# Reordering the per-block work of ScalarE and VectorE in the projection stage of a fused conditional-residual kernel

## Chip, cores and metric

The kernel runs on one core of one Trainium2 chip. The metric is the device time of one execution in microseconds. TensorE is PE, VectorE is DVE, ScalarE is ACT, GpSimd is POOL; SyncE (SP) issues most of the DMAs.

## The reference, cut to what matters

An activation `x` of shape (64, 32, 512) goes through four residual layers. The first three are small mixers. The fourth is paged attention with 32 query heads and 8 key and value heads of 128, and its projections are the stage that is changed:

```python
q = rmsnorm(x @ Wq.T) ; k = rmsnorm(x @ Wk.T) ; v = x @ Wv.T   # 4096, 1024 and 1024 columns
q, k = rope(q, pos), rope(k, pos)
o = softmax(q @ concat(k_cache, k).T / sqrt(128), masked) @ concat(v_cache, v)
x = x + o @ Wo.T
```

## The kernel before, in words

The program has three stages, one after the other: the mixers, the projections, and the attention. The function `projections` works on 16 tiles of 128 rows of `x`. Every tile is multiplied with 12 column blocks of 512: steps 0 to 7 are queries, 8 and 9 keys (steps 0 to 9 are those "with rotation", `ROT` = 10), and 10 and 11 values (`BLK` = 12). Numbers are kept as pairs of 16-bit parts, so a block costs 12 matmuls into one of four PSUM banks `blk` (L963 to L965).

Each engine has its own hand-written order, a loop over the steps n of a tile (`body`, L878, L955, L1024, L1110, L1226), and the engines meet at counting semaphores. What one block goes through:

- PE: the 12 matmuls; then `turn_heads` (L934), four transposes into a PSUM bank `tq` of heads that were finished two steps before. The heads turned at step n are query block n-2, and at steps 0 and 1 the two key blocks of the tile before. `tq` and its SBUF target `turned` have two buffers each, used in turn, so even steps and odd steps have one each. After block 10 PE runs `turn_x` (L923), which transposes the next tile's input.
- ACT: waits for block n, takes the row sums of squares (`squares`, L994, four instructions with accumulators at L999), and then in the same step copies the heads turned at step n-1 to `turned` as the high 16-bit part (`heads_high`, L986, executed at L979). Before that copy it waits until the DMA that stored the previous contents of the same `turned` buffer has landed (`out_q`). At even steps it splits a piece of the key cache, value cache or output weight (`chunk_high`, L1017). At steps 0 and 1 it scales the key blocks of the tile before (`normalise_keys`, L1003) before it waits for the block. At step 8 it makes the high part of the next tile's input (`x_high`, L981).
- DVE: waits for the squares of block n (both engines read the same PSUM bank, so one goes after the other), makes the two rotary products (`rotate`, L1208 and L1212), then the low part of the heads turned at step n-1 (`heads_low`, L1218), at odd steps the low part of the piece (`chunk_low`, L1223), one of eight small steps on the next tile's scales (`scale_step`, L1134), at step 9 `x_low` (L1163), and at step 10 `keep_xt` (L1168), which takes the transposed input out of PSUM. `mean` (L1172), a square root on ACT (L1028) and `inverse` (L1185 to L1194) close the tile.
- POOL: adds the two products (`add`, L1087), some work on the values (L1092, L1097), and at step 8 the tables of the next tile (L1071).
- SP: at even steps stores the piece whose `chunk_low` DVE made in the step before and loads another (`chunks`, L864; the store waits for `c_low`), and only then stores the heads turned at step n-2 (`store_heads`, L826). At step 9 it stores the values of the tile before (L847).

Of the kernel before, what the change touches and what calls it, by code (L numbers as in the profile page):

```python
# [696 lines left out]
def projections(nc, ident, ident16, up, cs, vw, cos, sin, wa, wb, wh, wl, first, v_idx, pages, wo_t, k_t, v_rows,  # L697
# [4 lines left out]
    with ctx:  # L702
# [36 lines left out]
        out_q = [sem(f"stored{i}") for i in range(2)]  # L739
        rest1, vmid, vlow, v_out = sem("v_rest"), sem("v_mid"), sem("v_low"), sem("v_stored")  # L740
        XSTEPS, CSTEPS, CHUNKS = 7, 4, 6

        keys0, query0, values0, fresh0, rscale0, page_row = first
        pages_in, early, early_values = sem("pages_in"), sem("first_sample"), sem("first_values")
# [58 lines left out]
        def is_tile(t, n):  # L803

            return isinstance(t, int) and t == n
# [113 lines left out]
        @block.tensor  # L919
        def _(pe):  # L920
            mm = nc.tensor.matmul

            def turn_x(t, p):  # L923

                pe.wait_ge(xhigh, t + 1)
                pe.wait_ge(xlow, t + 1)
                after(pe, xt_done, t)
                for k in range(KD):
                    for h, part in enumerate((xh, xl)):
                        at = (2 * k + h) * P  # L930
                        last = nc.tensor.transpose(xp[:, at:at + P], part[:, k * P:(k + 1) * P], ident16[:, :])
                last.then_inc(xturned, 1)

            def turn_heads(t, n):  # L934
                idx = t * ROT + n
                if n < QB:
                    pe.wait_ge(sum_done, idx + 1)
                    src = rn[n % NR]
                else:
                    pe.wait_ge(kn_done, t * KB + n - QB + 1)  # L940
                    src = kr[n - QB]
                after(pe, high, idx - 1)
                after(pe, low, idx - 1)
                for h in range(HB):
                    last = nc.tensor.transpose(tq[n % 2][:, h * P:(h + 1) * P], src[:, h * P:(h + 1) * P],
                                               ident[:, :])
                last.then_inc(tq_done, 1)

            def bank_free(t, n):
                if n < ROT:  # L950
                    pe.wait_ge(rot_done, t * ROT + n + 1)
                else:
                    pe.wait_ge(v_read, t * VB + n - ROT + 1)

            def body(t, p):  # L955
                pe.wait_ge(xt_done, t + 1)
                for n in range(BLK):
                    if unread(t, n):
                        bank_free(*unread(t, n))
                    out = blk[n % NB][:, :]  # L960
                    cols = slice(n * D, (n + 1) * D)
                    for k in range(KD):
                        mm(out, xt[p][:, k, 0, :], wh[:, k, cols], start=(k == 0), stop=False)  # L963
                        mm(out, xt[p][:, k, 0, :], wl[:, k, cols], start=False, stop=False)  # L964
                        last = mm(out, xt[p][:, k, 1, :], wh[:, k, cols], start=False, stop=(k == KD - 1))  # L965
                    last.then_inc(blk_done, 1)
                    if heads_at(t, n):
                        turn_heads(*heads_at(t, n))
                    if n == ROT and not is_tile(t, NT - 1):
                        turn_x(t + 1, 1 - p)  # L970

            turn_x(0, 0)
            tiles(pe, body)
            for n in range(QB, ROT):
                turn_heads(NT - 1, n)

        @block.scalar
        def _(act):
            copy = lambda out, in_, **kw: nc.scalar.activation(out, in_, ACT.Copy, **kw)  # L979

            def x_high(t, p):  # L981
                act.wait_ge(scaled, t + 1)
                after(act, xturned, t)
                copy(xh[:, :], x3[p][:, :], scale=col[p][:, 2:3]).then_inc(xhigh, 1)

            def heads_high(t, n):  # L986
                idx = t * ROT + n
                act.wait_ge(tq_done, idx + 1)

                after(act, out_q[n % 2], count(t, n) * 16)  # L990
                src, dst, _ = head_views(n)
                copy(dst, src).then_inc(high, 1)

            def squares(t, n):  # L994

                after(act, sq_done, t * ROT + n - 1)
                for h in range(HB):
                    at = h * QB + n if n < QB else HQ + (n - QB) * HB + h
                    last = nc.scalar.activation(square[n % 2][:, h, :], blk[n % NB][:, h * HD:(h + 1) * HD], ACT.Square,  # L999
                                                accum_out=ss[:, 0, at:at + 1])  # L1000
                last.then_inc(sq_done, 1)

            def normalise_keys(t, p, j):  # L1003
                act.wait_ge(sum_done, t * ROT + QB + j + 1)
                act.wait_ge(inv_done, t + 1)
                for h in range(HB):
                    cols = slice(h * HD, (h + 1) * HD)
                    at = HQ + j * HB + h
                    last = copy(kr[j][:, cols], kr[j][:, cols], scale=inv[p][:, at:at + 1])
                last.then_inc(kn_done, 1)  # L1010

            def middle(t, j):

                act.wait_ge(rest1, t * VB + j + 1)
                copy(vp[:, 1, j * D:(j + 1) * D], v32[j][:, :]).then_inc(vmid, 1)

            def chunk_high(t, c):  # L1017
                act.wait_ge(c_in[c % 3], t * (16 * CHUNKS // 3) + (c // 3 + 1) * 16)

                after(act, c_out[c % 3], t * (16 * CHUNKS // 3) + c // 3 * 16)  # L1020
                a, h, _ = chunk_views(c)
                copy(h, a, scale=up[:, c // 2:c // 2 + 1]).then_inc(c_high, 1)

            def body(t, p):  # L1024
                for n in range(BLK):
                    if n == BLK - 1:
                        act.wait_ge(root_in, t + 1)
                        nc.scalar.activation(ss[:, 2, :], ss[:, 1, :], ACT.Sqrt).then_inc(rooted, 1)  # L1028
                    if not is_tile(t, 0) and n < KB:
                        normalise_keys(t - 1, 1 - p, n)  # L1030
                    act.wait_ge(blk_done, t * BLK + n + 1)
                    if n < ROT:
                        if n == 0:
                            after(act, root_in, t)
                        squares(t, n)
                    if heads_at(t, n - 1):
                        heads_high(*heads_at(t, n - 1))
                    if not is_tile(t, 0) and n in (2, 4):
                        middle(t - 1, n // 2 - 1)
                    if n % 2 == 0:  # L1040
                        chunk_high(t, n // 2)
                    if n >= ROT:
                        j = n - ROT

                        after(act, v_out, t * 4 * 16)
                        after(act, vlow, t * VB)
                        copy(v32[j][:, :], blk[n % NB][:, :], scale=col[p][:, 6:7])
                        copy(vp[:, 0, j * D:(j + 1) * D], blk[n % NB][:, :], scale=col[p][:, 6:7]
                             ).then_inc(v_read, 1)
                    if n == ROT - 2 and not is_tile(t, NT - 1):  # L1050
                        x_high(t + 1, 1 - p)

            x_high(0, 0)
            tiles(act, body)
            for j in range(KB):
                normalise_keys(NT - 1, 1, j)
            for j in range(KB):
                heads_high(NT - 1, QB + j)
            for j in range(VB):
                middle(NT - 1, j)  # L1060
# [70 lines left out]
        def _(dve):  # L1131
# [93 lines left out]

            def body(t, p):  # L1226
                for n in range(BLK):
                    if n < ROT:
                        rotate(t, p, n)
                    if heads_at(t, n - 1):  # L1230
                        heads_low(*heads_at(t, n - 1))
                    if n % 2 == 1:
                        chunk_low(t, n // 2)
                    if not is_tile(t, NT - 1):
                        if n <= XSTEPS:
                            scale_step(t + 1, 1 - p, n)
                        if n == ROT - 1:
                            x_low(t + 1, 1 - p)
                        if n == ROT:
                            keep_xt(t + 1, 1 - p)  # L1240
                    if n == ROT:
                        mean(t, p)
                    if n == BLK - 1:
                        inverse(t, p)
# [462 lines left out]
```

## Time and profile before

| | us |
|---|---|
| median of 3 runs (2423.46 to 2427.11) | 2425.59 |
| the profiled execution, its own time | 2425.75 |
| its span, first to last instruction | 2424.1 |
| PE busy in the span | 2172.3 (90%) |
| DVE busy | 1985.7 (82%) |
| ACT busy | 1408.3 (58%) |
| POOL busy | 1042.5 (43%) |

The lines of the profile are read like this: the line number is that of the kernel file, then come the engine and the operation, "out<-in" by the program's buffer names, and the shape. Rows of a timeline begin with the start and the duration in us, and end, where the engine had been idle, with how long and what released it. PE's busy time is longer than its issue time, since matmuls overlap, so PE can wait although it shows as busy.

### The profile page before, as it was taken

The numbers are of one execution on the slowest core, as the hardware profiler recorded it, in microseconds if no ns is written. First come the engines' busy times: TensorE is split into PE (matmuls) and PEld (weight loads), VectorE is DVE, ScalarE is ACT, GpSimd is POOL, SyncE is SP. The second block draws the span as 40 slices with busy tenths as digits, with TensorE's granted clock in tenths as the row PEclk, the third lists the DMA queues.
The fourth block names the chain that finished last, engine by engine and source line by source line (L and its number), as shares of the span: only waits on it lengthen the run. The fifth ranks groups of instructions, "written<-read, shape, count | busy, mean of one in ns | idle before, by whom it ended". The sixth has DMA issues, their size and how long they took to land.

```text
span 2424.1 us, 61876 instructions
## 1 busy us (share of the span) xinstructions
PE 2172.3 (90%) x17328; PEld 1376.8 (57%) x17328; DVE 1985.7 (82%) x5085; ACT 1408.3 (58%) x4073; POOL 1042.5 (43%) x1329
## 2 busy tenths in 40 slices
PE   0886889899998975899999999999999999999998
PEld 0443444444444433666666666676676666766765
DVE  7786767767676766899998998998998998998995
ACT  0443666666666664566665665665665665665663
POOL 3343444444444443344444443443443444444442
PEclk9998999999999998999999999999999999999999
DMA  7884454545454559977777877877877777777771
GB/s 278 309 301 153 139 179 160 188 149 180 161 173 161 169 195 304 304 217 235 238 234 214 242 234 216 240 232 216 240 234 222 234 232 224 235 229 230 238 230 53
DMA packets 402151, 522.68 MB, mean 216 GB/s; under 512 B 50866, under 2 KB 297522, under 8 KB 399795
## 3 DMA queue, kind: packets, MB, share of 16 engines
q1 hardware_dynamic: 361010, 371.71, 48.9%
q0 software_dynamic: 40832, 147.34, 19.2%
q8 instruction: 135, 2.21, 0.4%
q14 instruction: 174, 1.42, 0.2%
HBM read 426.36 MB, written 92.54 MB: 214 GB/s over the span
## 4 chain that ended last, share of the span: by engine, by line
issue 26%; PE 20%; POOL 9%; DVE 4%; SPq 1%; POOLq 1%; DMA 1%; DVEq 0%; ACT 0%; ACTq 0%
PE att_y L1504 5%; PE att_scores L1464 5%; POOL wh L1410 4%; PE att_tr L1472 3%; POOL att_values L1401 3%; PE att_o L1492 2%; PE att_o L1493 2%; PE att_o L1494 2%; POOL wh L1401 1%; DVE att_prob L1590 1%; PE att_tr_new L1475 1%; POOL att_ot L1418 1%; DMA wh<-k_parts 1%; SPq L95 1%; DVE att_tpl L1613 1%
## 5 line engine op out<-in xcount | busy, mean ns | idle before, releaser
L1532 ACT ACTIVATE att_tph<-att_tr 128x512 f16<-128x512 f32 x512 | 305.8, 597 | 516.4 <-PE att_tr_new L1475 516.4
L1590 DVE CUSTOM_DVE_ANT_0 att_prob<-att_scores,att_mask 128x544 f32<-128x544 f32 x512 | 371.0, 725 | 106.7 <-PE att_scores L1465 65.6
L1410 POOL TENSOR_TENSOR wh<-att_prob,att_col 128x128 f32<-128x128 f32 x512 | 230.5, 450 | 524.7 <-DVE att_col L1601 500.2
L1504 PE MATMUL att_y<-att_wo,att_ot 128*128 128x512 f16 x1536 | 408.6, 380 | 5.9 <-DVE att_res L1630 5.9
L1613 DVE SCALAR_TENSOR_TENSOR att_tpl<-att_tr,att_tph 128x512 f16<-128x512 f32 x512 | 347.6, 679 | 2.5 <-ACT att_tph L1532 1.7
L1472 PE MATMUL att_tr<-ident,wh 128*128 128x128 f32 x2048 | 329.2, 284 | 0.8 <-DVE wh L1606 0.8
L1606 DVE TENSOR_SCALAR wh<-att_prob,att_col 128x512 f32<-128x512 f32 x512 | 327.5, 640 | 0.0
L1087 POOL TENSOR_TENSOR proj_rn<-proj_ra,proj_rb 128x512 f32<-128x512 f32 x128 | 162.7, 1271 | 320.2 <-DVE proj_rb L1212 320.2
L963 PE MATMUL proj_blk<-wh,proj_xt 128*128 128x512 f16 x768 | 294.8, 384 | 0.8 <-DVE proj_xt L1168 0.8
L964 PE MATMUL proj_blk<-wl,proj_xt 128*128 128x512 f16 x768 | 294.9, 384 | 0.0
L965 PE MATMUL proj_blk<-wh,proj_xt 128*128 128x512 f16 x768 | 294.9, 384 | 0.0
L1464 PE MATMUL att_scores<-wh 128*128 128x512 f16 x768 | 228.2, 387 | 51.6 <-PEq L702 20.4
L1208 DVE TENSOR_TENSOR proj_ra<-proj_blk,proj_ta 128x512 f32<-128x512 f32 x160 | 110.0, 687 | 180.2 <-ACT proj_square L999 180.2
L1418 POOL TENSOR_TENSOR att_ot<-att_of,att_ot 128x512 bf16<-128x512 f32 x128 | 158.4, 1238 | 225.3 <-DVE att_ot L1625 209.7
L1472 PEld LDWEIGHTS att_tr<-ident,wh 128*128 128x128 f32 x2048 | 217.6, 142 | 63.9 <-issue 2.8
L999 ACT ACTIVATE proj_square<-proj_blk 128x128 f32<-128x128 f32 x640 | 168.5, 278 | 130.8 <-PE proj_blk L965 130.5
L1536 ACT ACTIVATE att_prob<-att_prob,att_col,att_rscale 128x544 f32<-128x544 f32 x256 | 215.3, 841 | 32.8 <-DVE att_col L1596 20.7
L1536 ACT ACTIVATE att_prob<-att_prob,att_col,rscale 128x544 f32<-128x544 f32 x256 | 215.4, 841 | 27.8 <-DVE att_col L1596 18.6
L1464 PE MATMUL att_scores<-att_keys,att_query 128*128 128x512 f16 x768 | 220.9, 378 | 2.2 <-DVE att_col L1590 1.4
L1504 PEld LDWEIGHTS att_y<-att_wo,att_ot 128*128 128x128 bf16 x1536 | 153.8, 101 | 85.5 <-issue 9.5
L1492 PE MATMUL att_o<-att_tph,att_values 128*128 128x128 f16 x1024 | 188.9, 222 | 2.8 <-DMA att_values<-v_parts,att_idx 1.7
L1493 PE MATMUL att_o<-att_tpl,att_values 128*128 128x128 f16 x1024 | 188.7, 222 | 0.0
(195 smaller groups left out, 5329.4 us busy)
## 6 DMA issues: line engine op xcount, KB each, us to landing
wh<-k_parts SPq DMA_DIRECT2D x512, 128.0 KB, 4.3
att_keys<-k_parts SPq DMA_DIRECT2D x512, 128.0 KB
q_parts<-proj_turned SPq DMA_DIRECT2D x128, 256.0 KB, 2.9
v_new_parts<-proj_vp SPq DMA_DIRECT2D x64, 256.0 KB, 3.0
wh<-q_parts SPq DMA_DIRECT2D x32, 512.0 KB, 4.9
att_query<-q_parts SPq DMA_DIRECT2D x32, 512.0 KB
pro_ring<-in_w_t SPq DMA_DIRECT2D x12, 1024.0 KB, 8.3
mix_wraw<-in_w_t POOLq DMA_DIRECT2D x24, 512.0 KB, 5.6
```

Of the source, the lines that this page charges most:

```text
L963: mm(out, xt[p][:, k, 0, :], wh[:, k, cols], start=(k == 0), stop=False)
L964: mm(out, xt[p][:, k, 0, :], wl[:, k, cols], start=False, stop=False)
L965: last = mm(out, xt[p][:, k, 1, :], wh[:, k, cols], start=False, stop=(k == KD - 1))
L1410: g.tensor_tensor(norm[q][:, L:L + P].rearrange("p (a s) -> p a s", s=S), prob[q][:, cached(q)[1]].unsqueeze(1).to_broadcast([P, 4, S]), c ...
L1464: mm(old, a, k, start=start, stop=stop)
L1472: nc.tensor.transpose(tr[q][:, c * P:(c + 1) * P], norm[q][:, c * P:(c + 1) * P], ident[:, :])
L1504: last = mm(y_ps[:, :], ot[p][:, a, h, :], wo[:, h, w, :], start=(h == 0 and start), stop=(h == HQ - 1 and stop))
L1532: copy = lambda out, in_, **kw: nc.scalar.activation(out, in_, ACT.Copy, **kw)
L1536: nc.scalar.activation(prob[q][:, :], prob[q][:, :], ACT.Exp, bias=col[q][:, 1:2], scale=row_scale(i), accum_out=col[q][:, 2:3]).then_inc( ...
L1590: v.tensor_tensor_reduce(out=prob[q][:, :], in0=sc[q], in1=mask[bi % 2][:, at:at + LK], scale=1.0, scalar=-3.0e38, op0=ALU.add, op1=ALU.ma ...
L1606: v.tensor_scalar(out=norm[q][:, 0:L], in0=prob[q][:, cached(q)[0]], scalar1=col[q][:, 3:4], scalar2=None, op0=ALU.mult).then_inc(norm_don ...
L1613: v.scalar_tensor_tensor(out=tpl[q][:, :], in0=tr[q][:, :], scalar=TOP, in1=tph[q][:, 0:L], op0=ALU.mult, op1=ALU.subtract)
```

## The change

Three moves, and nothing is added or taken away. On ACT `heads_high` of step n-1 stands ahead of the wait for block n and its squares instead of behind them, and `x_high` of the next tile stands at step 5, in front of that wait, instead of at the end of step 8. On DVE `heads_low` stands ahead of `rotate`, two scale steps of the next tile are made in each of steps 0 to 3 instead of one in each of 0 to 7, `x_low` comes at step 6, and all of these stand ahead of `rotate`; `chunk_low` stays behind it. On PE `turn_x` follows block 9 instead of block 10.

```diff
+        XHIGH = 5
 ...
                     if heads_at(t, n):
                         turn_heads(*heads_at(t, n))
-                    if n == ROT and not is_tile(t, NT - 1):
+                    if n == ROT - 1 and not is_tile(t, NT - 1):
                         turn_x(t + 1, 1 - p)
 ...
                         normalise_keys(t - 1, 1 - p, n)
+                    if heads_at(t, n - 1):
+                        heads_high(*heads_at(t, n - 1))
+                    if n == XHIGH and not is_tile(t, NT - 1):
+                        x_high(t + 1, 1 - p)
                     act.wait_ge(blk_done, t * BLK + n + 1)
                     if n < ROT:
                         if n == 0:
                             after(act, root_in, t)
                         squares(t, n)
-                    if heads_at(t, n - 1):
-                        heads_high(*heads_at(t, n - 1))
 ...
-                    if n == ROT - 2 and not is_tile(t, NT - 1):
-                        x_high(t + 1, 1 - p)
 ...
                 for n in range(BLK):
-                    if n < ROT:
-                        rotate(t, p, n)
                     if heads_at(t, n - 1):
                         heads_low(*heads_at(t, n - 1))
-                    if n % 2 == 1:
-                        chunk_low(t, n // 2)
                     if not is_tile(t, NT - 1):
-                        if n <= XSTEPS:
-                            scale_step(t + 1, 1 - p, n)
-                        if n == ROT - 1:
+                        for step in range(2 * n, min(2 * n + 2, XSTEPS + 1)):
+                            scale_step(t + 1, 1 - p, step)
+                        if n == XHIGH + 1:
                             x_low(t + 1, 1 - p)
                         if n == ROT:
                             keep_xt(t + 1, 1 - p)
+                    if n < ROT:
+                        rotate(t, p, n)
+                    if n % 2 == 1:
+                        chunk_low(t, n // 2)
                     if n == ROT:
                         mean(t, p)
```

## Rows read from the trace of the kernel before

**Rows 1.** Windows; columns: stretch, us, busy us (instructions) per engine, PE clock, DMA.
```profile
228.00:859.00 631.00, 569.81 (x2871) 278.55 (x2872) 439.84 (x790) 403.69 (x1667) 285.80 (x270) 0.98 0.50 165
```
**Rows 2.** Waits from 228 to 899 us; columns: total us, times, longest.
```profile
DVE proj_ra L1208 <- ACT proj_square L999: 180.2, 97, 6.6
...
ACT proj_turned L979 <- DMA q_parts<-proj_turned: 34.6, 49, 2.1
PE proj_xp L931 <- issue: 32.5, 15, 2.3
...
ACT proj_turned L979 <- DMA k_new_parts<-proj_turned: 22.0, 15, 1.8
```
**Rows 3.** Tiles proj_xp, proj_xh and line L1223; columns: ns minimum/median/maximum, first and last start.
```profile
L1168 DVE COPY proj_xt<-proj_xp x16: 691/692/693, 227.2 to 856.9; 128x1024 f16<-128x1024 f16 x16
...
L979 ACT ACTIVATE proj_xh<-proj_x,proj_col x16: 710/744/753, 224.5 to 849.8; 128x512 f16<-128x512 f32 x16
...
L1223 DVE SCALAR_TENSOR_TENSOR proj_chunk_parts<-proj_chunk,up,proj_chunk_parts x96: 739/1214/1465, 238.3 to 897.6; 128x512 f16<-128x512 f32 x96
```
**Rows 4.** Timeline of one tile, steps 5 to 9: from one stored piece to the next.
```profile
590.80 1.38 DVE L1223 SCALAR_TENSOR_TENSOR proj_chunk_parts<-proj_chunk,up,proj_chunk_parts 128x512 f16<-128x512 f32 x1
...
592.21 0.33 SPq L861 DMA_DIRECT2D v_parts<-proj_chunk_parts  x1
...
593.41 1.24 SPq L839 DMA_DIRECT2D q_parts<-proj_turned  x2
...
596.25 0.60 ACT L979 ACTIVATE proj_turned<-proj_tq 128x512 f16<-128x512 f32 x1 [0.74 <-DMA q_parts<-proj_turned]
...
596.88 0.69 DVE L1218 TENSOR_TENSOR proj_turned<-proj_tq,proj_turned 128x512 f16<-128x512 f32 x1
...
597.49 1.24 DVE L1223 SCALAR_TENSOR_TENSOR proj_chunk_parts<-proj_chunk,up,proj_chunk_parts 128x512 f16<-128x512 f32 x1
...
602.97 0.60 ACT L979 ACTIVATE proj_turned<-proj_tq 128x512 f16<-128x512 f32 x1 [0.77 <-DMA q_parts<-proj_turned]
```
**Rows 5.** Timeline: squares, products and sum of step 7, transposes of steps 8 and 9.
```profile
594.37 0.28 ACT L999 ACTIVATE proj_square<-proj_blk 128x128 f32<-128x128 f32 x1 [1.27 <-PE proj_blk L965]
...
595.54 0.69 DVE L1208 TENSOR_TENSOR proj_ra<-proj_blk,proj_ta 128x512 f32<-128x512 f32 x1 [0.68 <-ACT proj_square L999]
...
596.15 0.68 DVE L1212 TENSOR_TENSOR proj_rb<-proj_blk,proj_tb 128x512 f32<-128x512 f32 x1
...
596.91 1.27 POOL L1087 TENSOR_TENSOR proj_rn<-proj_ra,proj_rb 128x512 f32<-128x512 f32 x1 [0.95 <-DVE proj_rb L1212]
...
597.72 0.63 PE L945 MATMUL proj_tq<-ident,proj_rn 128*128 128x128 f32 x4 [0.26 <-DVE proj_turned L1218]
...
600.79 0.63 PE L945 MATMUL proj_tq<-ident,proj_rn 128*128 128x128 f32 x4
```
**Rows 6.** Timeline of the same tile, steps 2 and 3: the first heads.
```profile
579.92 1.12 SPq L839 DMA_DIRECT2D k_new_parts<-proj_turned  x2
...
583.02 0.60 ACT L979 ACTIVATE proj_turned<-proj_tq 128x512 f16<-128x512 f32 x1 [1.28 <-DMA k_new_parts<-proj_turned]
```
**Rows 7.** Timeline of the same tile: its first steps, and steps 9 to 0 of the next.
```profile
570.80 0.63 PE L945 MATMUL proj_tq<-ident,proj_kr 128*128 128x128 f32 x4
...
572.44 1.28 ACT L979 ACTIVATE proj_kr<-proj_kr,proj_inv 128x128 f32<-128x128 f32 x4
...
601.05 0.28 ACT L999 ACTIVATE proj_square<-proj_blk 128x128 f32<-128x128 f32 x1 [0.63 <-PE proj_blk L965]
...
606.90 0.69 DVE L1168 COPY proj_xt<-proj_xp 128x1024 f16<-128x1024 f16 x1
...
607.51 0.23 DVE L1172 TENSOR_SCALAR proj_ss<-proj_ss,proj_col 128x40 f32<-128x40 f32 x1
...
609.79 0.16 DVE L1194 TENSOR_TENSOR proj_inv<-proj_ss 128x8 f32<-128x8 f32 x1
...
611.97 0.66 PE L945 MATMUL proj_tq<-ident,proj_kr 128*128 128x128 f32 x4
```

## The prediction

> **What bounds the kernel now.** The change touches one stage, so I first cut the trace to it. In the windows view the steady part of the projections lasts 631 us, with PE busy 570, DVE 440, ACT 404 and POOL 286 [rows 1]. No engine is full, so what matters is who waits for whom. The copy of the transposed input gives the cadence: L1168 runs 16 times from 227.2 to 856.9, so a tile takes 629.7 / 15 = 41.98 us [rows 3]. PE alone could do better: two successive transposes of heads with a full block between them, in a stretch where nothing held the second, start 3.07 us apart (597.72 to 600.79) [rows 5]. Ten such steps and two blocks without transposes would be some 36 us. So about 6 us a tile are waiting.
>
> The list of waits shows where. PE stands 32.5 us in 15 waits, 2.2 us a tile, ahead of the transposes of the next input (L931) [rows 2]. DVE waits 180 us for the squares, and ACT 34.6 + 22.0 us for the DMA that stores turned heads [rows 2]. The DMA waits are the ones to look at, since they repeat with a period of their own. I followed one even step to the next in the timeline [rows 4]: the low part of the piece, L1223, ends at 590.80 + 1.38 = 592.18. SP, which had been waiting for it, stores the piece at 592.21, loads another, and only then, at 593.41, stores the heads. That store lands and lets ACT take the next even heads at 596.25. DVE follows at 596.88, L1223 at 597.49 to 598.73, and the next heads leave at 602.97. Hence a loop of 602.97 - 596.25 = 6.72 us for two steps, against 2 x 3.07 = 6.14 us for PE. **This loop of stores, not PE, sets the pace of the steady steps**, and PE shows it: its transposes at 597.72 had waited 0.26 us for the low part of the heads [rows 5]. The squares are outside the loop, because they stand ahead of the head copy on ACT: in the same step the squares began at 594.37, 1.9 us before the copy at 596.25 [rows 4, 5].
>
> **The change, part by part.** I write S for the start of a step's squares and H for the start of the copy of heads in front of them in the new order. All instructions stay, so only order counts.
>
> *Heads ahead of the squares (ACT).* ACT works in order. The copy H still waits for the store of the heads two steps back, and now the squares are queued behind that wait, and behind the squares the products on DVE, and behind those L1223, and behind L1223 on SP the store that the next H waits for. The loop is closed through the squares. Its length:
> - S to the first product 595.54 - 594.37 = 1.17; to the second 0.61; DVE is free again after another 0.61 (as between 596.88 and 597.49); L1223 at its undisturbed 0.74 [rows 3 to 5]. Together 3.13 us from S to the end of L1223. The low part of the heads costs nothing here: it runs beside the squares (0.69 us against 1.17).
> - End of L1223 to H: 596.25 - 592.18 = 4.07 in one loop and 602.97 - 598.73 = 4.24 in the next [rows 4]; I take 4.15. For the first pair the store is that of keys, whose issue to copy is 583.02 - 579.92 = 3.10 against 596.25 - 593.41 = 2.84 [rows 4, 6], so 4.4.
> - H to the squares 0.60 [rows 4].
>
> That is 3.13 + 4.15 + 0.60 = **7.88 us for two steps, where 6.72 stand now**; 8.13 for the pair with the keys' store. PE's 6.14 hides under it, as does POOL's sum (1.27) with the transposes behind it.
>
> *The input's high part at step 5* (`x_high`) stands between a late H and the squares of step 5. Its 0.74 [rows 3] was beside PE's work before; now it is in the loop once per tile. 7.88 + 0.74 = 8.62.
>
> *From the tile's first transposes to the squares of step 1*: the key scaling starts at 572.44 and takes 1.28 as now, and then the heads of step 0 leave (0.60) ahead of the squares: 574.3 - 570.80 = 3.5 us [rows 7].
>
> *From the squares of step 1 to those of step 9*: 8.13 + 8.62 + 7.88 + 7.88 = 32.5 us.
>
> *The end of the tile.* Today the squares of step 9 start at 601.05 and the first transposes of the next tile at 611.97, 10.9 us later, with PE's wait of 2.2 us for the input inside [rows 7, 2]. In the new order the input has been split since step 6 and is turned after block 9, so this wait goes. What is late next is the copy of the input out of PSUM: DVE does products and L1223 of step 9 (3.13 after S), the low heads (0.61), the copy (0.61 to the next start, 606.90 to 607.51), so `mean` starts at 4.4. `Mean` to the end of `inverse` is 609.95 - 607.51 = 2.44, then comes the key scaling at 1.28 and some 0.1 of hand-over: 8.2 us after S [rows 7]. PE's next block starts when the copy is done, at about 4.4, and ends at 7.0, so the key scaling ends last. **The tile's end gains 2.7 us.**
>
> *Scale steps by two, and the low part of the input at step 6* cost nothing as long as they run while DVE waits for squares. Without that cover the low part adds its own duration, 0.74 like L1223's minimum, once a tile; the even step it is in has over a microsecond free.
>
> Sum for a tile: 3.5 + 32.5 + 8.2 = 44.2 against 41.98, +2.2 us. Fourteen full tiles: +31. The first tile has no keys' store ahead of it and so one loop less, about 0. In the last tile (whose input part at step 5 falls away) there is no input wait to win back: today its squares of step 9 come 30.25 us after the first transposes (601.05 - 570.80) [rows 7], in the new order 3.5 + 31.8 = 35.3, so +5. Together +36 on the profiled execution's 2425.75: **2462 us**. Its span lies 1.7 us under that, and the time 0.2 us above the median of the runs, so nothing is to be corrected.
>
> **The price from both sides.** L1223 can be 0.74 or up to 1.47 [rows 3]. In the rows it is long when POOL's sum runs: POOL from 596.91 to 598.18, L1223 until 598.73, some 0.55 after POOL's end [rows 4, 5]. In these rows the two did not overlap. In the new order L1223 comes right behind the second product, 0.61 after its start, and POOL's sum 0.76 after it; L1223 would be first by 0.15 us. I take it as first, with POOL's sum half a microsecond later, under cover. If POOL wins, L1223 ends 0.76 + 1.27 + 0.55 = 2.58 after the second product rather than 1.35: +1.23 in each of four loops. For the store's landing the rows give 2.84 to 3.10.
>
> The Trainium skill (SBUF — State Buffer, "Who interferes with whom") says of the port that DVE and POOL share that issue order decides who blocks, and the first holds it for its whole instruction. By that rule L1223 keeps its 0.74 and the sum stays 2462; by the longest measured duration it would be the second rival. The rows before agree with the rule for the POOL-first order alone.
>
> A difference under 0.2%, about 5 us, cannot be told from no change.
>
> **The rivals.**
> 1. *POOL gets the port first.* 1.23 x 4 = 4.9 us a tile, x 16 = 79: 2541. Against it are the 0.15 us above; for it, that this lead is small. 8%.
> 2. *The opposite sign: the head copies are never late.* Then the squares keep today's spacing and the tile's end gains 2.7 us x 15 = 40: 2385. This needs the store to land before the block is done: from the end of L1223 only 6.14 - 3.13 - 0.60 = 2.4 us remain, and 4.07 is the shortest I saw. For it: stores issued at another moment meet other transfers, and DMA is busy only half of the time [rows 1]. 11%.
> 3. *Loss and gain cancel.* Shortening each of four loops by 0.55 us takes the 2.2 us away, i.e. a way from L1223 to copy of 3.6 us: about 2425. 7%.
> 4. *The clock.* The mean granted clock of the stage is 0.98 of 2.4 GHz [rows 1], so little time is spent at the lower level of 1.2 GHz. In the new order PE idles over a microsecond in every second step, and if that brought more time at the lower level, a block of 2.6 us would cost as much again at most; most of it lies under the loop. It would add up to 30 us and stays inside my forecast's own range.
>
> **How the numbers follow.** The loop through the squares, with port and clock uncertain, has 74%, and 2440 to 2495 as its own range. Faster is rival 2, 12% with a part of rival 3; same is the rest of rival 3, 6%; slower is the loop and rival 1, 82%. The range 2424 to 2510 leaves out rivals 1 and 2.
>
> **What would show it.** In the changed profile the wait of PE ahead of L931 is gone; ACT's waits for the stores of heads grow from 57 us to well over 100, and the squares start right behind a head copy at steps 3, 5, 7 and 9; the head copies of even steps are 7.9 us apart (today 6.72); L1223 takes 0.74 in most places; the copy L1168 is spaced by about 44 us. If the copies are 6.2 us apart and L1168 by less than 40, the store was never in the way and I am wrong. If L1223 stays at 1.2 or more, rival 1 holds.

## The result, and the profile after

The changed kernel takes **2470.38 us** (median of 4 runs, 2466.41 to 2475.03) against 2426.05 us, a ratio of 1.0185 with a 95% interval of 1.0165 to 1.0205: 44 us slower, where 36 us slower (2462 us) had been forecast. The time lies inside the stated range of 2424 to 2510 us. The profiled execution has a span of 2467.8 us.

The three windows below are those of the projections' steady part, of the last tile with the tail, and of the rest, in the changed kernel.

```profile
226.90:888.80 661.90, 567.75 (x2873) 280.57 (x2874) 411.73 (x787) 390.22 (x1665) 310.38 (x270) 0.99 0.47 156
888.80:939.60 50.80, 40.37 (x192) 20.23 (x192) 28.21 (x53) 31.47 (x126) 22.11 (x17) 0.93 0.46 158
939.60:2467.80 1528.20, 1435.99 (x13824) 1011.39 (x13824) 1339.20 (x3795) 899.21 (x2179) 650.94 (x963) 0.98 0.76 228
```

The steady part took 631 us [rows 1] and takes 662 now; PE, DVE and ACT are busy for as long as before or less. POOL's busy time alone grew, from 286 to 310 us. So the time is waiting. The list of waits from 228 to 945 us says for whom:

```profile
DVE proj_turned L1219 <- ACT proj_turned L980: 196.5, 80, 5.4
ACT proj_turned L980 <- DMA q_parts<-proj_turned: 191.7, 59, 6.1
...
DVE proj_ra L1209 <- ACT proj_square L1000: 62.7, 93, 5.9
PE proj_tq L946 <- DVE proj_turned L1219: 47.1, 40, 3.6
...
ACT proj_turned L980 <- DMA k_new_parts<-proj_turned: 36.7, 15, 2.7
```

ACT's wait for the stores of turned heads went from 34.6 + 22.0 [rows 2] to 191.7 + 36.7 = 228 us. The wait of PE ahead of the transposes of the next input, 32.5 us before [rows 2], is not in the list any more. The change took away the wait it was aimed at, and it made the wait for the stores four times as long.

Next the two tiles views, with the copy of the transposed input and the low part of the pieces, to be held against [rows 3]:

```profile
L1169 DVE COPY proj_xt<-proj_xp x16: 677/679/691, 226.1 to 888.0; 128x1024 f16<-128x1024 f16 x16
...
L1224 DVE SCALAR_TENSOR_TENSOR proj_chunk_parts<-proj_chunk,up,proj_chunk_parts x96: 739/742/745, 237.3 to 932.4; 128x512 f16<-128x512 f32 x96
...
L1088 POOL TENSOR_TENSOR proj_rn<-proj_ra,proj_rb x128: 1261/1450/1714, 234.8 to 924.1; 128x512 f32<-128x512 f32 x128
```

A tile takes (888.0 - 226.1) / 15 = 44.13 us instead of 41.98. The low part of the piece is never longer than 745 ns, and POOL's sum is longer instead (median 1450 ns, 1267 before).

The timeline of steps 5 to 9 of one tile shows the loop, in the place of [rows 4, 5]:

```profile
602.88 0.60 ACT L980 ACTIVATE proj_turned<-proj_tq 128x512 f16<-128x512 f32 x1 [3.60 <-DMA q_parts<-proj_turned]
...
603.98 0.27 ACT L1000 ACTIVATE proj_square<-proj_blk 128x128 f32<-128x128 f32 x1
604.35 0.63 PE L946 MATMUL proj_tq<-ident,proj_rn 128*128 128x128 f32 x4 [1.31 <-DVE proj_turned L1219]
...
605.15 0.69 DVE L1209 TENSOR_TENSOR proj_ra<-proj_blk,proj_ta 128x512 f32<-128x512 f32 x1 [0.95 <-ACT proj_square L1000]
605.76 0.68 DVE L1213 TENSOR_TENSOR proj_rb<-proj_blk,proj_tb 128x512 f32<-128x512 f32 x1
606.36 0.74 DVE L1224 SCALAR_TENSOR_TENSOR proj_chunk_parts<-proj_chunk,up,proj_chunk_parts 128x512 f16<-128x512 f32 x1
606.52 1.71 POOL L1088 TENSOR_TENSOR proj_rn<-proj_ra,proj_rb 128x512 f32<-128x512 f32 x1 [3.65 <-DVE proj_rb L1213]
607.12 0.33 SPq L862 DMA_DIRECT2D v_parts<-proj_chunk_parts  x1
...
608.33 0.98 SPq L840 DMA_DIRECT2D q_parts<-proj_turned  x2
611.22 0.60 ACT L980 ACTIVATE proj_turned<-proj_tq 128x512 f16<-128x512 f32 x1 [3.46 <-DMA q_parts<-proj_turned]
...
618.96 0.60 ACT L980 ACTIVATE proj_turned<-proj_tq 128x512 f16<-128x512 f32 x1 [3.98 <-DMA q_parts<-proj_turned]
619.45 0.27 ACT L1000 ACTIVATE proj_square<-proj_blk 128x128 f32<-128x128 f32 x1
623.09 0.68 DVE L1169 COPY proj_xt<-proj_xp 128x1024 f16<-128x1024 f16 x1
...
627.54 0.66 PE L946 MATMUL proj_tq<-ident,proj_kr 128*128 128x128 f32 x4 [0.88 <-ACT proj_kr L980]
```

Read it from the top: the copy of heads starts once the old store has landed, after 3.6 us in which ACT did nothing; then the squares, the products, the low part of the piece, its store, the store of the heads, and again a copy that waited 3.46 us. From copy to copy it is 8.34 us with the input's high part in between, and 7.74 us in the next pair.

Not all of the 44 us is here. The attention stage starts with L1464 at 923.8 us before and with L1465 at 958.1 after, and the rest to the end of the span is 1500.3 and 1509.7 us:

```profile
L1464 PE MATMUL att_scores<-wh x768: 376/377/634, 923.8 to 2366.9; 128*128 128x512 f16 x192
...
L1630 DVE SCALAR_TENSOR_TENSOR att_res<-att_y,oscale,att_res x16: 750/751/752, 1112.1 to 2420.8; 128x512 f32<-128x512 f32 x16
```
```profile
L1465 PE MATMUL att_scores<-wh x768: 376/377/634, 958.1 to 2412.1; 128*128 128x512 f16 x192
...
L1631 DVE SCALAR_TENSOR_TENSOR att_res<-att_y,oscale,att_res x16: 750/751/752, 1144.9 to 2464.4; 128x512 f32<-128x512 f32 x16
```

The first fence is the kernel before, the second the changed one. The projections cost 34.3 us more and the attention, of which no line was changed, 9.4 us. Between the first and the last residual sum of the attention (`att_res`) it is 1308.7 us before and 1319.5 after.

### The profile page after: what moved, and what is told of

It is laid out like the page before. It is cut to its first block, busy times and chain, and to the rows that moved or that the text cites. A ratio compares the mean times of both kernels' runs of the same rounds, so it can differ in the third digit from the quotient of the medians.

```text
span 2467.8 us, 61864 instructions
## 1 busy us (share of the span) xinstructions
PE 2176.4 (88%) x17328; PEld 1381.6 (56%) x17328; DVE 1956.0 (79%) x5085; ACT 1396.7 (57%) x4073; POOL 1070.5 (43%) x1329
## 4 chain that ended last, share of the span: by engine, by line
issue 27%; PE 17%; POOL 9%; DVE 6%; POOLq 1%; SPq 1%; DMA 1%; DVEq 0%; ACT 0%
PE att_y L1505 5%; PE att_scores L1465 4%; POOL wh L1411 4%; POOL att_values L1402 3%; PE att_tr L1473 3%; DVE att_prob L1591 2%; POOL wh L1402 1%; PE att_o L1493 1%; PE att_o L1495 1%; PE att_o L1494 1%; PE att_tr_new L1476 1%; DVE att_tpl L1614 1%; POOL att_ot L1419 1%; DVE wh L1607 1%; DVE att_tph L1617 1%
## 5 line engine op out<-in xcount | busy, mean ns | idle before, releaser
L1591 DVE CUSTOM_DVE_ANT_0 att_prob<-att_scores,att_mask 128x544 f32<-128x544 f32 x512 | 370.8, 724 | 121.0 <-PE att_scores L1466 50.5
L1088 POOL TENSOR_TENSOR proj_rn<-proj_ra,proj_rb 128x512 f32<-128x512 f32 x128 | 189.3, 1479 | 322.4 <-DVE proj_rb L1213 310.4
L1465 PE MATMUL att_scores<-wh 128*128 128x512 f16 x768 | 226.6, 385 | 51.5 <-PEq L702 19.9
L1219 DVE TENSOR_TENSOR proj_turned<-proj_tq,proj_turned 128x512 f16<-128x512 f32 x160 | 109.9, 687 | 196.5 <-ACT proj_turned L980 196.5
L1465 PE MATMUL att_scores<-att_keys,att_query 128*128 128x512 f16 x768 | 222.2, 379 | 5.2 <-DMA att_keys<-k_parts 3.7
L980 ACT ACTIVATE proj_turned<-proj_tq 128x512 f16<-128x512 f32 x160 | 97.1, 607 | 229.0 <-DMA q_parts<-proj_turned 191.7
```

Of the source, the lines that this page charges most:

```text
L1465: mm(old, a, k, start=start, stop=stop)
L1591: v.tensor_tensor_reduce(out=prob[q][:, :], in0=sc[q], in1=mask[bi % 2][:, at:at + LK], scale=1.0, scalar=-3.0e38, op0=ALU.add, op1=ALU.ma ...
```

## Experiments

Two theories stood against each other for the projections: that a loop through the store of the heads, now with squares and products in it, sets the pace; or that the input's earlier split, or slow stores as such, are to blame. Four kernels came first, and the others followed from what they left open. The names of lines are those of the changed kernel; the kernel before has them one lower, and the kernels with added waits have the attention's two or three higher.

**SP's order in the changed kernel.**

```diff
                 for n in range(BLK):
-                    if n % 2 == 0:
-                        chunks(t, n // 2)
...
                     if heads_at(t, n - 2):
                         store_heads(*heads_at(t, n - 2))
+                    if n % 2 == 0:
+                        chunks(t, n // 2)
```

> The changed kernel with one edit on SP: at even steps the turned heads are stored before the piece, so their store no longer waits for L1224. Theory of the loop: from H the low heads end 1.3 us later, the store leaves at once and lands in 2.9 us, so the next copy could start 4.3 us after H, under PE's 6.14 us for two steps. The squares come on time, ACT's waits for the stores of heads fall from 228 us to under 30, a tile takes 36.5 to 38.5 us instead of 44.1, and the kernel 2426 - 15 x 4.5 = about 2355 us (2340 to 2385). Rival (the stores themselves are slow, by crowded DMA engines, and the order on SP is beside the point): waits and time stay near 2470, at most 10 us less.

Measured: 2350.56 us, ratio to before 0.9702 (0.9676 to 0.9729), some 120 us under the changed kernel with not one instruction more or less. The tiles view and the waits from 228 to 899 us:

```profile
L1169 DVE COPY proj_xt<-proj_xp x16: 678/680/692, 227.0 to 773.5; 128x1024 f16<-128x1024 f16 x16
```
```profile
ACT proj_turned L980 <- DMA q_parts<-proj_turned: 25.0, 43, 1.9
ACT proj_turned L980 <- DMA k_new_parts<-proj_turned: 12.0, 15, 2.4
```
```profile
575.32 1.88 SPq L840 DMA_DIRECT2D q_parts<-proj_turned  x2
575.89 0.60 PE L946 MATMUL proj_tq<-ident,proj_rn 128*128 128x128 f32 x4
...
578.13 0.60 ACT L980 ACTIVATE proj_turned<-proj_tq 128x512 f16<-128x512 f32 x1 [0.59 <-DMA q_parts<-proj_turned]
578.91 0.60 PE L946 MATMUL proj_tq<-ident,proj_rn 128*128 128x128 f32 x4
```

A tile takes 546.5 / 15 = 36.43 us, near the 36 us of PE's work, and PE's transposes are 578.91 - 575.89 = 3.02 us apart. The waits fell to 37 us, a little more than the 30 expected. Slow stores are ruled out: a store issued at 575.32 still let its copy start only at 578.13, 2.8 us later, as before, and it is when they are issued that counts.

**The same edit on the kernel before.**

> The kernel before with the same edit on SP alone. Theory: the loop of 6.72 us for two steps goes, steps run at PE's 3.07, and the 2.2 us wait for the next input stays: (6.72 - 6.14) x 4 = 2.3 us a tile less, 39.7 us a tile, about 2391 us (2380 to 2405). Rival (slow stores): 2426 within 5 us.

Measured: 2404.05 us, ratio 0.9926 (0.9898 to 0.9953). The direction is that of the loop, the size is below it: a tile takes (837.9 - 227.2) / 15 = 40.71 us, 1.3 less instead of 2.3. The waits for stores are nearly gone (6.4 and 0.2 us), but PE still waits 30.3 us ahead of the input's transposes. The rows of this kernel show why the gain is small:

```profile
573.74 0.63 PE L945 MATMUL proj_tq<-ident,proj_rn 128*128 128x128 f32 x4
...
576.21 0.68 DVE L1218 TENSOR_TENSOR proj_turned<-proj_tq,proj_turned 128x512 f16<-128x512 f32 x1
...
577.04 0.63 PE L945 MATMUL proj_tq<-ident,proj_rn 128*128 128x128 f32 x4
...
578.86 0.68 DVE L1212 TENSOR_TENSOR proj_rb<-proj_blk,proj_tb 128x512 f32<-128x512 f32 x1
579.45 0.68 DVE L1218 TENSOR_TENSOR proj_turned<-proj_tq,proj_turned 128x512 f16<-128x512 f32 x1
...
580.28 0.63 PE L945 MATMUL proj_tq<-ident,proj_rn 128*128 128x128 f32 x4
```

With no store in the way the transposes are still 3.30 and 3.24 us apart, 6.54 us for two steps and not 6.14. They start 0.15 us after the low heads have ended (576.21 + 0.68 = 576.89, then 577.04), and the low heads stand behind the products. So the old order holds a second loop, from PE's block over squares, products and low heads back to PE's transposes, a little shorter than the loop of stores. No run tests it by itself, but with the low heads ahead of the products, in the kernel above, the steps are at 3.02 us. The loop of stores in the kernel before is not much longer: its copies of even steps came at 583.02, 589.24, 596.25 and 602.97 [rows 4, 6], in the mean 6.65 us apart. The second of them is this row:

```profile
589.24 0.60 ACT L979 ACTIVATE proj_turned<-proj_tq 128x512 f16<-128x512 f32 x1 [0.27 <-DMA q_parts<-proj_turned]
```

**The input's moves alone** (the changed kernel with the heads back where they were):

```diff
-                    if heads_at(t, n - 1):
-                        heads_high(*heads_at(t, n - 1))
                     if n == XHIGH and not is_tile(t, NT - 1):
...
                         squares(t, n)
+                    if heads_at(t, n - 1):
+                        heads_high(*heads_at(t, n - 1))
...
-                    if heads_at(t, n - 1):
-                        heads_low(*heads_at(t, n - 1))
...
                         rotate(t, p, n)
+                    if heads_at(t, n - 1):
+                        heads_low(*heads_at(t, n - 1))
```

> The changed kernel with the head copies back behind the squares on ACT and the low heads back behind the products on DVE: what is left is the earlier splitting and turning of the next input. Theory: the loop is the old one, 6.72 us for two steps, and only the 2.2 us wait ahead of the input's transposes goes, of which 1.5 to 2.2 us a tile reach the end: 2426 - 25 = about 2400 us (2390 to 2410). Rival (the input's moves are what makes the change slow, by holding ACT and DVE in front of a block): 2440 or more.

Measured: 2417.33 us, ratio 0.9984 (0.9967 to 1.0001), so no difference clear of noise, and above the expected range (2390 to 2410). The projections did gain: (833.7 - 225.3) / 15 = 40.56 us a tile, 21 us over 15 tiles. The attention took 13 us back (1322.0 us between its residual sums against 1308.7), which is the miss. The input's moves are not what makes the change slow.

**The heads' moves alone** (on the kernel before):

```diff
+                    if heads_at(t, n - 1):
+                        heads_high(*heads_at(t, n - 1))
                     act.wait_ge(blk_done, t * BLK + n + 1)
...
                         squares(t, n)
-                    if heads_at(t, n - 1):
-                        heads_high(*heads_at(t, n - 1))
...
+                    if heads_at(t, n - 1):
+                        heads_low(*heads_at(t, n - 1))
                     if n < ROT:
                         rotate(t, p, n)
-                    if heads_at(t, n - 1):
-                        heads_low(*heads_at(t, n - 1))
```

> The kernel before with the heads' moves alone (copy ahead of the wait for the block on ACT, low part ahead of the products on DVE). Theory: the loop goes through the squares, 7.9 us for two steps, and the wait for the input at the end of the tile stays, so this is at least as slow as the whole change: 2470 to 2490 us, head copies of even steps 7.9 us apart. Rival (the input's moves are to blame): 2426 or less.

Measured: 2518.13 us, ratio 1.0402 (1.0365 to 1.0439): slower than the whole change by 48 us, more than the 20 allowed for. Head copies of even steps came at 577.72, 585.68, 593.37 and 601.28, 7.9 us apart as expected. What was too small was the price of the input at the end of the tile. In this kernel PE waits for it after block 10, by the timeline

```profile
606.66 0.22 PE L931 MATMUL proj_xp<-ident,proj_xh 128*128 128x128 f16 x1 [4.57 <-issue]
```

4.57 us and not 2.2: the low part of the input is behind a later step 9 on DVE, and took 1.75 us beside POOL's sum. The clock has a part in it too. The matmuls behind this wait start 0.43 us apart instead of 0.22, and the granted clock of the stage is 0.94 where the changed kernel has 0.99:

```profile
607.14 0.63 PE L963 MATMUL proj_blk<-wh,proj_xt 128*128 128x512 f16 x1
607.57 0.63 PE L964 MATMUL proj_blk<-wl,proj_xt 128*128 128x512 f16 x1
```
```profile
607.10:610.50 3.40, 3.40 (x11) 1.26 (x9) 2.79 (x10) 0.24 (x1) 0.00 (x0) 0.51 0.79 293
228.00:949.00 721.00, 594.86 (x2871) 288.12 (x2870) 433.14 (x793) 392.73 (x1668) 308.61 (x267) 0.94 0.44 145
```

Eight matmuls of that block take 3.4 us and not 1.7, and over the stage PE is busy for 595 us against 568 in the changed kernel, for the same matmuls. How much of these 27 us reached the end was not measured. The input's moves thus earn more inside the whole change than alone: they take away a wait which the heads' moves would have doubled.

**Which order, ACT's or DVE's.** Two kernels from the changed one: the low heads behind the products again (ACT's order is left), or the head copy behind the squares again (DVE's order is left).

```diff
-                    if heads_at(t, n - 1):
-                        heads_low(*heads_at(t, n - 1))
...
                         rotate(t, p, n)
+                    if heads_at(t, n - 1):
+                        heads_low(*heads_at(t, n - 1))
```

> The changed kernel with the low heads back behind the products on DVE, the head copy staying ahead of the squares on ACT. Theory: ACT's order alone closes the loop through the squares, and with the low heads between the products and L1224, POOL's sum now starts first and holds L1224 until 0.55 us after its end: 1.17 + 0.61 + 0.76 + 1.27 + 0.55 = 4.36 us from the squares to the end of L1224 instead of 3.13, so 9.1 us for two steps, 5 us a tile more than the change: 2540 us (2515 to 2560). Rival (ACT's order is harmless, DVE's does the damage): near 2420.

Measured: 2562.02 us, ratio 1.0562 (1.0536 to 1.0588), 2 us above the expected range. Here too the granted clock of the stage is 0.94, which the estimate had not counted. The price was worked out from POOL getting ahead, and both show: head copies at 595.70 and 604.72, 9.02 us apart, and L1224 at its long duration:

```profile
L1224 DVE SCALAR_TENSOR_TENSOR proj_chunk_parts<-proj_chunk,up,proj_chunk_parts x96: 737/1380/1468, 240.5 to 1029.0; 128x512 f16<-128x512 f32 x96
```

The other half:

```diff
-                    if heads_at(t, n - 1):
-                        heads_high(*heads_at(t, n - 1))
                     if n == XHIGH and not is_tile(t, NT - 1):
...
                         squares(t, n)
+                    if heads_at(t, n - 1):
+                        heads_high(*heads_at(t, n - 1))
```

> The changed kernel with the head copy back behind the squares on ACT, the low heads staying ahead of the products on DVE. Theory: the squares leave the loop but the products are in it: copy to low heads 0.63, 0.61 to the products, 1.22 for these, 0.74 for L1224, then 4.15 to the next copy, 7.35 us for two steps, between the 6.72 of before and the 7.88 of the change: 2440 us (2425 to 2455). Rival (DVE's order is harmless): near 2417, as with the input's moves alone; rival (DVE's order does all the damage): 2470.

Measured: 2465.95 us, ratio 1.0182 (1.0145 to 1.0219), a miss on the high side: as slow as the whole change. The loop is as short as expected (copies at 602.75, 610.12 and 617.57, 7.4 us apart), but the tile still takes (880.7 - 226.3) / 15 = 43.63 us. The estimate had left out the first pair, which runs from 594.83 to 602.75, 7.9 us. A further part is likely that the products of steps 2 and 9 now wait for a copy behind the squares; it was not measured apart. So either order closes a loop of its own: it takes both in their old places, or the store of the heads set free of the products, by SP's order as above or by DVE's as below.

**The piece ahead of the products** (the changed kernel, SP as it is):

```diff
                         heads_low(*heads_at(t, n - 1))
+                    if n % 2 == 1:
+                        chunk_low(t, n // 2)
...
-                    if n % 2 == 1:
-                        chunk_low(t, n // 2)
```

> The changed kernel with L1224, the low part of the piece, directly behind the low heads and ahead of the products on DVE; SP keeps its order. Theory: the store of the piece stays ahead of the store of the heads but no longer waits for squares and products: copy to low heads 0.63, 0.61, 0.74 for L1224, 4.15 to the next copy, 6.1 us for two steps, no more than PE's 6.14. Waits for stores of heads fall by more than half, a tile takes 37 to 39 us and the kernel about 2365 us (2350 to 2395). Rival (only SP's order counts): 2450 or more.

Measured: 2372.21 us, ratio 0.9776 (0.9743 to 0.9809); a tile takes (800.5 - 232.0) / 15 = 37.9 us. ACT's waits for the stores fell from 228 to 97.6 + 21.2 = 119 us, a little less than the half expected. With SP's order untouched, taking squares and products out of the loop is worth 98 us. The two kernels that open the loop in two different places both end far below the kernel before. That is the loop shown, not argued.

**The attention stage.** All kernels so far with the input's moves had the longer attention, and DVE's program in them, as built, is 2375 instructions long, in the others 2377. Waits on semaphores that have their value long before were put in once, ahead of DVE's first tile. In the built program the three waits are two instructions more here, and one more in the kernel before:

```diff
             keep_xt(0, 0)
+            dve.wait_ge(xlow, 1)
+            dve.wait_ge(xhigh, 1)
+            dve.wait_ge(scaled, 1)
             tiles(dve, body)
```

> The changed kernel with three waits that are long satisfied, once, on DVE ahead of its first tile; they bring DVE's program of 2375 instructions back to the 2377 of the kernel before. It asks about the attention stage, which the change does not touch: from the first to the last instruction of L1630 or L1631 it took 1308.7, 1308.3 and 1308.6 us in the three kernels with 2377 DVE instructions, and 1319.5, 1319.7 and 1322.0 in the three with 2375. Theory (where DVE's loop of the attention lies in its program sets a stall of instructions): 1308 to 1311 us there, and the kernel at 2458 to 2462. Rival (something else in the moved input work, or chance): 1319 to 1322 us there and the kernel near 2470.

Measured: 2459.14 us, ratio 1.0133 (1.0109 to 1.0156), 11 us under the changed kernel, with tiles of (891.7 - 229.3) / 15 = 44.16 us as before the edit. The residual sums, and DVE's waits without a releaser in this kernel's attention (from 1200 to 2440 us), then those of the changed kernel (from 1145 to 2465 us):

```profile
L1634 DVE SCALAR_TENSOR_TENSOR att_res<-att_y,oscale,att_res x16: 750/751/753, 1151.1 to 2458.6; 128x512 f32<-128x512 f32 x16
...
DVE att_mask L1579 <- issue: 13.1, 6, 2.8
DVE att_prob L1594 <- issue: 0.4, 2, 0.2
```
```profile
DVE att_prob L1591 <- issue: 30.0, 45, 4.5
DVE att_mask L1576 <- issue: 11.5, 6, 2.6
```

1307.5 us between the first and last residual sum, and the 30 us of waits at L1591 are gone. Two more kernels were run once each: the changed kernel with two of the three waits (2376 instructions), and the kernel before with all three (2378):

> The changed kernel with two satisfied waits, 2376 DVE instructions. One look at the same span: 1308 us or 1316 and more places the step between 2375 and 2377. The projections keep 44.1 us a tile.

> The kernel before with three satisfied waits once on DVE, so that its program has 2378 instructions, one more than before. One look at the attention's span from the first to the last residual sum. If only positions of 2375 stall (a boundary crossed by the shorter program), it stays at 1308 us; if every length but 2377 stalls, it is 1316 or more. The projections keep 42.0 us a tile either way.

With 2376 the attention took 2466.1 - 1145.1 = 1321.0 us and DVE stood still before L1578 for 34.0 us in 6 waits; with 2378 it took 2416.5 - 1112.0 = 1304.5. The single times were 2471.04 and 2421.52 us, and the tiles took 44.0 and 42.0 us. By these single runs the step is between 2376 and 2377 instructions.

**Both findings together**: the changed kernel with SP's order and the three waits.

> The changed kernel with both findings: SP stores the turned heads ahead of the piece, and DVE's program is brought to 2377 instructions by satisfied waits. If both effects are what they seem and add up: tiles at 36.4 us as with SP's order alone, the attention's L1630 to L1634 rows spanning 1308 us instead of 1319.7, the kernel 2350.6 - 11 = 2340 us (2335 to 2346). If the attention's stall belongs to something else: 2350.

Measured: **2335.61 us**, ratio to before 0.9643 (0.9626 to 0.966), the fastest of all: tiles of (775.9 - 228.9) / 15 = 36.5 us and an attention of 2337.3 - 1029.2 = 1308.1.

```profile
ACT proj_turned L980 <- DMA q_parts<-proj_turned: 26.8, 43, 2.5
ACT proj_turned L980 <- DMA k_new_parts<-proj_turned: 11.0, 15, 2.4
```

## Why the prediction was right, and where it was off

- **What bounds the kernel.** The loop of stores, 6.72 us for two steps, was said to set the pace. SP's order on the kernel before takes its waits away, but gains 1.3 us a tile and not 2.3. Two sizes were off. The 6.72 us is one pair of steps, and the mean of three pairs in that tile is 6.65. And PE's own pace, 3.07 us a step, is not what the old order falls back to without the waits for stores: it runs at 3.27, since another loop, of 6.54 us, lay close under the loop of stores.
- **The loop through squares and products.** Forecast 7.88 us; the rows show 7.74, and 8.34 with the input's high part in it where 8.62 was forecast. Its parts fit: squares to first product 1.17 us; squares to the end of L1224 607.10 - 603.98 = 3.12 (3.13 forecast); from there to the next copy 4.12 (4.15); copy to squares 0.49 where 0.60 was taken, since ACT starts its next instruction before the last has ended.
- **The end of the tile.** 627.54 - 619.45 = 8.09 us against the 8.2 forecast.
- **The tile.** 44.13 us in the mean against 44.2. The tile shown takes less: its first transposes are at 584.16 and the squares of step 1 at 587.42, so with 619.45 - 587.42 = 32.03 up to those of step 9 it is 3.26 + 32.03 + 8.09 = 43.38 us where 3.5 + 32.5 + 8.2 stood. Each term is a little too long for this tile, and that the mean is met to 0.1 us is in part luck.
- **Port between DVE and POOL.** L1224 came first by 0.16 us (606.36 against 606.52) and kept its 0.74 everywhere. POOL's sum took 1.71 us instead of 1.27 and so paid 0.44 us, which stayed under cover. The rows before showed POOL first only; the changed kernel shows DVE first, and now both orders agree with what the Trainium skill (SBUF — State Buffer, "Who interferes with whom") says, that who issues first blocks the other. In the kernel with ACT's order alone, POOL is first again (598.73 against 599.17), and L1224 takes 1.38 us instead of 0.74. That is about half of what a loop is longer there (9.02 us against 7.74); the other 0.6 us are the low heads between the products and L1224.
- **Rivals.** POOL first (2541, once called "the second rival" in the prediction) did not come. Its mechanism showed in the kernel with ACT's order alone, which ran at 2562. That head copies are never late (2385) failed in the changed kernel; with SP's order it is nearly so, at 2351. In the changed kernel the clock moved little: 0.99 in the steady windows, 0.93 in the last tile with the tail. In the two slower kernels, the heads' moves alone and ACT's order alone, it fell to 0.94 over the stage.
- **The term that was missing.** The sum held +36 us for the projections and nothing for what follows; they gave +34.3, and 9.4 came from the attention, through DVE's program being two instructions shorter. The step that failed is that the prediction put nothing for the stages behind the one it changed; "All instructions stay, so only order counts" was the sentence: the computing instructions stay, the waits between them are laid down differently. With the length restored the kernel is at 2459, 32 to 35 us over before (ratio 1.0133, medians 2459.14 and 2424.55), near the 36 forecast.

## What to carry to other kernels

Before a step is moved ahead of a wait, write down the loop that the wait belongs to: which buffer, which store, and what the queue that issues this store is itself waiting for. Here the store of the heads stood behind a store that depended on DVE's last work of the step, and the move put the squares and products into that loop; two lines moved on SP turned 44 us of loss into some 72 us of gain (ratio 0.9702). Neither part does it alone: SP's order without the moves gave 18 us (ratio 0.9926). And look at the stages that a change does not touch: a few us there can be an effect of the program's length, which satisfied waits can test cheaply.

## What was not expected of the hardware

With 2375 or 2376 instructions in DVE's program the attention took 1315.5 to 1322.0 us between its residual sums in seven kernels; with 2377 or 2378 it took 1304.5 to 1308.7 in six. In the long ones DVE stands still with no releaser in the profile: the longest such wait is 4.0 to 5.2 us with 2375 instructions (at L1591) and 6.0 us with 2376 (at the line of the mask). In the short ones it is 3.0 us at most. The changed kernel's timeline has such a place about once in two tiles, of which this is one:

```profile
1320.95 0.43 DVE L1626 CAST att_ot<-att_of 128x512 bf16<-128x512 f32 x1
1323.31 0.66 DVE L1576 TENSOR_SCALAR att_mask<-att_iota,lens_f 128x512 f32<-128x512 f16 x1 [1.93 <-issue]
1327.98 0.72 DVE L1591 CUSTOM_DVE_ANT_0 att_prob<-att_scores,att_mask 128x544 f32<-128x544 f32 x1 [4.02 <-issue]
```

The profile lists 179 packets on the queue q14, of kind "instruction", in all seven kernels with the long attention, and 173 or 174 in all six with the short one. That DVE waits for its own code there is likely by this, and not shown. Which position in the program makes the stall stays open.
